# Moving the reciprocal of a head's denominators into the sums of the head before

## The reference

```python
def _L0_xattn_ref(query_input, source_input, Wq, Wk, Wv, Wo, proj, training):
    ratio = 1.0 / float(np.sqrt(proj.shape[0]))
    # _relu_kernel(x, proj) = relu(ratio * einsum('blhd,md->blhm', x, proj)) + 0.001
    qp = _relu_kernel(q, proj)
    kp = _relu_kernel(k, proj)
    kvs = jnp.einsum('blhm,blhd->bhmd', kp, v)
    num = jnp.einsum('blhm,bhmd->blhd', qp, kvs)
    ks_sum = jnp.sum(kp, axis=1)
    den = jnp.einsum('blhm,bhm->blh', qp, ks_sum)
    att = num / den[..., None]
    return jnp.einsum('blhd,hdk->blk', att, Wo)
x = x + _L0_xattn_ref(_layernorm(x, axis=-1), ctx_1024, ..., 0)
x = x + _L0_ffn_ref(_layernorm(x, axis=-1), ...)
```

## Time and profile before

| what | value |
|---|---|
| runs | 311.74, 311.84, 313.47 us |
| median | 311.84 us |
| profiled execution: span from the first to the last instruction | 276.2 us |
| median less the span | 35.6 us |
| busy in the span: tensor engine (matmul) | 247.8 us, 90% |
| vector engine | 190.4 us, 69% |
| scalar engine | 164.0 us, 59% |
| pool engine | 124.3 us, 45% |

### The profile page before, as it was taken

One profiled execution on the slowest core, in us unless ns is written; L12 is line 12 of the kernel. 1 busy time (PEld: TensorE's weight loads), 2 busy tenths in 40 slices (PEclk: granted clock), 3 DMA queues, 4 the chain that ended last, 5 costly groups with the idle time before them and its releaser, 6 DMA issues.

```text
span 276.2 us, 5724 instructions
## 1 busy us (share of the span) xinstructions
PE 247.8 (90%) x1697; PEld 211.5 (77%) x1697; DVE 190.4 (69%) x713; ACT 164.0 (59%) x343; POOL 124.3 (45%) x183
## 2 busy tenths in 40 slices
PE   7899999999999999989998999988899979999600
PEld 4658676676888999879977997967789979999600
DVE  4777759589658988988898888999877312222115
ACT  3566466465577777677776677755365646656400
POOL 5648899841101000217220732064256777777710
PEclk9999999999999999999999999999999999999965
DMA  6999999960004000001000100014779399984157
GB/s 203 280 244 198 198 203 196 194 92 0 2 1 152 2 0 2 2 0 54 26 4 0 48 31 2 2 39 153 194 209 298 122 269 298 343 252 117 41 189 266
DMA packets 38445, 34.03 MB, mean 123 GB/s; under 512 B 3581, under 2 KB 31234, under 8 KB 38288
## 3 DMA queue, kind: packets, MB, share of 16 engines
q1 hardware_dynamic: 35312, 28.96, 44.0%
q0 software_dynamic: 2272, 4.24, 4.4%
q10 hardware_dynamic: 832, 0.49, 0.6%
HBM read 19.80 MB, written 14.32 MB: 124 GB/s over the span
## 4 chain that ended last, share of the span: by engine, by line
PE 59%; DVE 24%; DMA 6%; issue 4%; POOL 3%; SPq 2%; ACT 1%; DVEq 0%; POOLq 0%; ACTq 0%
DVE X L922 11%; PE num L1184 10%; PE bank L1269 10%; PE bank L1145 5%; PE num L1279 5%; PE num L1123 5%; PE num L245 3%; PE num L247 3%; PE bank L245 3%; PE num L246 3%; PE bank L1087 3%; PE bank L246 2%; PE bank L247 2%; DMA wo_sb<-in_wo 2%; DVE X L1038 2%
## 5 line engine op out<-in xcount | busy, mean ns | idle before, releaser
L922 DVE SCALAR_TENSOR_TENSOR X<-num,rden,X 128x128 f32<-128x128 f32 x256 | 72.1, 344 | 6.6
L1184 PEld LDWEIGHTS num<-kvw_sb,q 128*128 128x128 f32 x512 | 65.9, 190 | 12.1 <-ACT q L583 5.7
L1184 PE MATMUL num<-kvw_sb,q 128*128 128x130 f32 x512 | 68.7, 277 | 3.6 <-DVE X L922 3.6
L666 ACT ACTIVATE relu_z<-bank 128x512 f32<-128x512 f32 x64 | 38.2, 596 | 21.6 <-PE bank L247 21.5
L546 POOL DMA_INDIRECT dispatched<-rows,slot_i x32 | 31.3, 977 | 41.1 <-DVE rows L988 32.6
L566 POOL DMA_INDIRECT expert_out<-yo,xb x39 | 38.2, 978 | 14.1 <-issue 9.1
L583 ACT ACTIVATE q<-relu_z 128x512 f32<-128x512 f32 x64 | 40.4, 632 | 6.7 <-DVE acc L841 0.8
L1269 PE MATMUL bank<-xT,wgu_sb 128*128 128x128 f32 x312 | 41.5, 276 | 0.0
L1022 DVE TENSOR_TENSOR hid<-bank,silu_g 128x256 f32<-128x256 f32 x39 | 16.5, 423 | 35.5 <-ACT silu_g L691 35.1
L1269 PEld LDWEIGHTS bank<-xT,wgu_sb 128*128 128x128 f32 x312 | 38.0, 192 | 0.1
L245 PE MATMUL bank<-y2T_hi,feat_hi 128*128 128x512 f32 x64 | 30.4, 475 | 0.2
(11 more groups left out here) (173 smaller groups left out, 402.5 us busy)
## 6 DMA issues: line engine op xcount, KB each, us to landing
wgu_sb<-in_wgu SPq DMA_DIRECT2D x39, 256.0 KB, 3.4
dispatched<-pad_row SPq DMA_DIRECT2D x3, 2795.0 KB, 32.7
xb<-dispatched SPq DMA_DIRECT2D x39, 65.0 KB, 3.5
y_back<-expert_out SPq DMA_DIRECT2D x4, 512.0 KB, 4.8
wd_sb<-in_wd SPq DMA_DIRECT2D x1, 1024.0 KB, 4.8
out<-X SPq DMA_DIRECT2D x4, 256.0 KB, 2.4
X<-in_x SPq DMA_DIRECT2D x3, 256.0 KB, 5.8
expert_out<-yo,xb POOLq DMA_INDIRECT x39, 4.0
```

The lines of the kernel that those rows point to most:

```text
L666: a.activation(relu_z[:, k % 2, :], z_bank[k % 2], ACT.Relu).then_inc(relu_done, 1)
L922: v.scalar_tensor_tensor(tile_of(n, t), banks[:, t // 2, t % 2, 0:P], rden[:, h % 2, t:t + 1], tile_of(n, t), ALU.mult, ALU.add).then_inc( ...
L1184: nc.tensor.matmul(num[:, 2 * (h % 2) + t // 2, HA * (t % 2):HA * (t % 2 + 1)], q[:, h % 4, part], kvw_h, start=True, stop=True).then_inc( ...
```

## The change

The reciprocal leaves the head of `weighted_sum` and becomes a function of its own, `denominators(f)`, with its wait for the four numerators. It is issued for head f+1 behind the second sum of head f (`DVE_NEXT` = 1, counted from 0); head 0's stands in front of its own sums. The single wait for all sums of the head before becomes one wait per tile, for the same tile's sum of the head before. Nothing changes on the other engines.

```diff
+        DVE_NEXT = 1
...
+            def denominators(f):
+
+                dve.wait_ge(num_done, f * TPB + TPB)
+                banks = num[:, 2 * (f % 2):2 * (f % 2) + 2, 0:2 * HA].rearrange("p b (t c) -> p b t c", t=2)
+                v.reciprocal(rden[:, f % 2, :].rearrange("p (b t) -> p b t", t=2), banks[:, :, :, P]).then_inc(rden_done, 1)
+
             def weighted_sum(n, h):
 
                 f = n * H + h
-                dve.wait_ge(num_done, f * TPB + TPB)
-                banks = num[:, 2 * (h % 2):2 * (h % 2) + 2, 0:2 * HA].rearrange("p b (t c) -> p b t c", t=2)
-                v.reciprocal(rden[:, h % 2, :].rearrange("p (b t) -> p b t", t=2), banks[:, :, :, P]).then_inc(rden_done, 1)
-                wait_past(dve, att_done, f * TPB)
+                banks = num[:, 2 * (f % 2):2 * (f % 2) + 2, 0:2 * HA].rearrange("p b (t c) -> p b t c", t=2)
+                if f == 0:
+                    denominators(0)
                 dve.wait_ge(rden_done, f + 1)
                 for t in range(TPB):
-                    v.scalar_tensor_tensor(tile_of(n, t), banks[:, t // 2, t % 2, 0:P], rden[:, h % 2, t:t + 1], tile_of(n, t),
+                    wait_past(dve, att_done, (f - 1) * TPB + t + 1)
+                    v.scalar_tensor_tensor(tile_of(n, t), banks[:, t // 2, t % 2, 0:P], rden[:, f % 2, t:t + 1], tile_of(n, t),
                                            ALU.mult, ALU.add).then_inc(att_done, 1)
+                    if t == DVE_NEXT and f + 1 < NB * H:
+                        denominators(f + 1)
```

## The result

The kernel after takes 323.13 us (median of 4 runs, 319.38 to 325.04) beside 311.79 of the kernel before: ratio 1.032, 95% interval 1.025 to 1.040. It is slower, as forecast, but by 11.3 us between the medians, or 10 by the ratio, where 5.5 were forecast, and outside the range.

What follows compares the result with a forecast made beforehand. Neither engine alone was taken as the attention stage's bound: tensor and vector engine lead by turns. Three batches at 1.95 us (5.85) and about -0.05 in the last, taken as 5.5, on 311.84 gave 317.3 us; range 310.5 to 321.5.

Steps and rivals of the forecast that it cites:

- about 35.6 us lie around the span: Whole kernel: 311.84 us median less the profile's span of 276.2 lies outside the span, untouched by the change.
- The loop: Attention stage: freed numerators, reciprocal and sums 3 and 4 form a cycle; no head in a row under 1.49 us.
- The batch, step by step: Heads 16 to 23: late moments, stalls and late top-2 search delay head 23's numerators by 1.95 us; three batches, 5.85.
- 1.95 - 0.87 - 0.05: Attention stage: 1.95 us loss per batch, 0.87 later moments within it, about -0.05 for the rest of the last batch.
- the idle time ahead of the rank matmuls: Tensor engine, done with head 21 by 120.48, stands idle 1.06 us until the rank matmuls at 121.54.
- The slot of 0.08: Vector engine: a reciprocal with another head's sum behind it takes only 0.08 us; ends 0 and 0.28.
- The third rival: Vector engine: the slot is not short, the reciprocal takes 0.28 us wherever it stands; 325.9 us, chance 0.10.
- The waits per tile: Sums 2 to 4 each get a wait on the head before's same-tile sum, long fulfilled, priced at 0.
- My upper end: Price of a fulfilled wait at most 0.11 us, the gap between the reciprocal's end and its first sum.
- The rival that the vector engine gains on all heads: The 27 or so heads that the vector engine leads gain 0.20 us each, -5.4, so 306.4 us; chance 0.09.
- the loss is taken up in the tail: Stalls partly absorbed, expert weights and rows getting a head start in the tail; centre 313 us, chance 0.16.

Runs made afterwards that it cites:

- k = 14, 15 and 0 to 4: Reciprocal moved into the middle of the head before only for these heads of each batch, the others starting with their own: 318.85 us, 1.027 against the kernel before.

## Why the prediction was wrong

- **The step that failed** is "about 35.6 us lie around the span (311.84 median less 276.2 [...]), and the change does not touch them". About 2 us lie around it (1.7 to 2.2 in every run with both numbers). The other 32 or so are time inside the span that the one trace did not have, 13.3 of it in the attention stage as waits for late signals, and the change made those 3.8 us longer. With the 5.6 of the terms that I did work out this gives 9.4, against 9.3 between the two profiled spans (317.7 and 308.4), 10 by the ratio and 11.3 between the medians; what the medians have beyond 9.4 is not taken apart. That 9.4 and 9.3 agree so closely is in part luck: the stage happened to begin 0.53 us earlier in the profile of the kernel after (82.21 against 82.74), and its end took 0.4 longer. The trace of before could have warned: the same kernel cannot spend a tenth of its time outside its first and last instruction without a name for it, and I gave it none.
- **The loop** was right: 1.49 forecast, 1.49 measured, and under the tensor engine's 1.58, with 0.09 to spare, it costs next to nothing without late signals (0.49 in all). What I did not see is that the spare is also what takes up a disturbance. With the reciprocal in the middle, the tensor engine stops at half a head, 1.15 us of work ahead in place of 2.30, and the vector engine cannot catch up at 1.32. The two places shown above fit this; that it makes all of the 3.8 us is argued, not shown.
- **The batch, step by step** was right to 0.04 us in seven steps, 1.95 forecast, 1.95 and 1.98 measured in the first two batches without scatters (30.76 - 28.81, 30.84 - 28.86). The last one has 0.82 (30.41 - 29.59) where the sum gives 1.95 - 0.87 - 0.05 = 1.03, since its 0.87 already stands in the moments that it begins with. One sum was off without consequence: head 21 is done at 118.01 + 1.58 + 1.05 = 120.64 and not 120.48, so the idle time ahead of the rank matmuls comes to 0.90, not 1.06; 0.88 was measured.
- **The slot of 0.08** was 0.10 (reciprocal at 110.03, the next sum at 110.13). The third rival, a price of 0.28 wherever the reciprocal stands, is out. Here a sum started 0.10 us after the start of a reciprocal of 0.18. By the rule that the prediction took from the Trainium skill ("VectorE: DVE Perf Modes", section "The DRAIN you can't avoid"), that the next operation is not issued until the pipe is empty, it could not have. But the same section adds, which the prediction left out, that a next operation that is not held starts earlier, and with that sentence the trace agrees.
- **The waits per tile** I priced at 0; alone they gain 0.07 us a head where the vector engine leads, 1.9 us in all. With the reciprocal moved no sum follows it fresh, so the 5.6 holds no second gain of this kind. My upper end had the right row (the 0.11 behind the reciprocal) and the wrong sign.
- **The rival that the vector engine gains on all heads** is out: idle time ahead of the reciprocal 37.9 us, and 20.7 without the scatters. That the loss is taken up in the tail is out too: from the last moments to the end 97.5 us (220.24 to 317.7) against 97.1 (211.34 to 308.4).

What stays open: why the tensor engine's signals come late while the pool engine issues indirect transfers. That leaving out these transfers takes them away is shown in four kernels, by which way the transfers bring them is not, nor why one execution had the transfers and no late signal. Why k = 14, 15 and 0 to 4 pay about 2 us more under them than without, though the scatters fall on later heads, was not tried.

## What to carry to other kernels

An instruction that is pulled ahead takes its wait with it: ask which results, already computable, now stand behind that wait, and whether the engine waited for feeds on just these; then add up the loop. A time that no row of the profile explains is not a constant; before it is carried over, look whether the run and the trace are the same kind of execution. And slack between two engines that looks idle in a smooth trace can be what takes up the disturbances of another execution.

## What the runs showed of the hardware

- By the records, signals of the tensor engine reached the scalar and the vector engine late, by 2.82 us in the kernel before, 3.03 in the kernel after and up to 6.2 with the tile waits alone (features that end at 195.35, relu at 201.52), in the attention stage only while the pool engine issued indirect transfers or right behind them: 13.7 us of the attention stage in the kernel before, none in it when the 24 scatters are left out.
- One of the executions, the first profiled one of the kernel before, had the scatters and no late signal in that stage: span 276.2 against 308.4.
- The granted clock fell behind a stand of 2.62 us (0.91 over 20 us) and not behind one of 1.57 (1.00).
- A sum that stood behind two waits that both came true late started 0.28 us after the reciprocal's start, behind one 0.21 to 0.22, and a sum of another head 0.10; four sums with a long fulfilled wait each took 1.13 us, as without.
